# Inputs of a state-space scan: multiplied from replicated token rows on ScalarE and GpSimd in place of TensorE outer products

## What is computed

```python
xc = silu(conv(xa) + conv_b)
Bm = xc @ B_w.T + B_b
Cm = xc @ C_w.T + C_b
A = -exp(clip(A_log, -5, 2))
def step(s, t):
    x_t, b_t, c_t = t
    s = clip(s * A + b_t[:, None, :] * x_t[:, :, None], -10, 10)
    return s, sum(c_t[:, None, :] * s, axis=-1)
```

## Time and profile before

| what | us |
|---|---|
| median of three runs | 1893.89 |
| the profiled execution | 1896.1 |
| its span | 1894.3 |
| TensorE, weight loads | 1524.7 busy, 80% |
| ScalarE | 522.2 busy, 28% |
| GpSimd | 240.0 busy, 13% |
| DMA | 72.65 MB, mean 38 GB/s |

### The profile page before, as it was taken

How to read it: one execution, slowest core, us unless ns; L and a number is a source line. 1 busy time by engine, 2 the same in 40 slices (tenths; PEclk the granted TensorE clock), 3 DMA queues, 4 the chain that set the end, 5 groups by cost and what they waited for, 6 DMA issues and landing times.

```text
span 1894.3 us, 57377 instructions
## 1 busy us (share of the span) xinstructions
PE 1783.8 (94%) x18024; PEld 1524.7 (80%) x18024; DVE 1583.7 (84%) x5997; ACT 522.2 (28%) x1130; POOL 240.0 (13%) x517
## 2 busy tenths in 40 slices
PE   5748779999999999999999999999999999999997
PEld 3434658888888889888888888898888888888886
DVE  5658978989898999989898989899898989898522
ACT  4532103232222223132322223231313232222322
POOL 1010012020111111020202011111102020111100
PEclk9769879999999999999999999999999999999999
DMA  6943100101010101001010101010100101010000
GB/s 191 318 143 108 28 14 14 28 18 31 21 30 20 25 15 36 15 20 30 15 31 21 30 20 30 14 32 15 30 21 18 29 18 31 21 30 9 1 7 6
DMA packets 103435, 72.65 MB, mean 38 GB/s; under 512 B 65384, under 2 KB 95616, under 8 KB 102656
## 3 DMA queue, kind: packets, MB, share of 16 engines
q1 hardware_dynamic: 101936, 67.56, 12.8%
q10 hardware_dynamic: 1232, 1.58, 0.3%
HBM read 45.50 MB, written 23.59 MB: 36 GB/s over the span
## 4 chain that ended last, share of the span: by engine, by line
PE 82%; DVE 1%; issue 1%; ACT 0%; POOL 0%; DVEq 0%; POOLq 0%; ACTq 0%
PE bank L1275 29%; PE bank L1262 24%; PE bank L1176 6%; PE bank L1191 5%; PE bank L1403 3%; PE bank L1350 3%; PE bank L1209 2%; PE bank L1364 2%; PE bank L1357 1%; PE bank L1337 1%; PE bank L1229 1%; PE bank L1383 1%; PE bank L1414 1%; PE bank L1393 1%; DVE x L1759 0%
## 5 line engine op out<-in xcount | busy, mean ns | idle before, releaser
L1646 DVE CUSTOM_DVE_ANT_0 state<-decayed_state,bank 128x128 f32<-128x128 f32 x2048 | 508.3, 287 | 53.4 <-PE bank L1176 48.0
L1636 DVE TENSOR_TENSOR decayed_state<-state,decay 128x128 f32<-128x128 f32 x2048 | 507.1, 287 | 7.6 <-issue 4.2
L1275 PE MATMUL bank<-f_w_sb,hs_whole 128*128 128x256 f32 x2048 | 486.5, 381 | 1.0 <-ACT hs_whole L1058 1.0
L1275 PEld LDWEIGHTS bank<-f_w_sb,hs_whole 128*128 128x128 f32 x2048 | 372.1, 190 | 49.4 <-ACT hs_whole L1058 5.8
L1058 ACT ACTIVATE hs_whole<-bank,f_b_sb 128x256 f32<-128x256 f32 x512 | 214.6, 471 | 650.2 <-PE bank L1262 650.2
L1176 PE MATMUL bank<-xrows,brows 128*128 128x256 f32 x1024 | 252.8, 336 | 39.4 <-DVE state L1646 23.1
L1176 PEld LDWEIGHTS bank<-xrows,brows 128*128 128x128 f32 x1024 | 170.1, 193 | 81.6 <-issue 46.2
L869 POOL TENSOR_TENSOR m_ve<-m_mv,m_eps 128x2 f32<-128x2 f32 x96 | 20.2, 211 | 1237.0 <-DVE m_mv L1673 1237.0
L1262 PE MATMUL bank<-fT_parts,f_w_hi 128*128 128x256 f32 x1024 | 171.2, 290 | 0.7 <-ACT fT_parts L1028 0.7
L1262 PE MATMUL bank<-late_fT_parts,f_w_hi 128*128 128x256 f32 x1024 | 171.5, 290 | 0.0
L1262 PEld LDWEIGHTS bank<-fT_parts,f_w_hi 128*128 128x128 f32 x1024 | 138.4, 189 | 14.0 <-issue 7.0
(11 more groups left out here) (166 smaller groups left out, 2313.3 us busy)
## 6 DMA issues: line engine op xcount, KB each, us to landing
brows<-bs_dram SPq DMA_DIRECT2D x1020, 2.0 KB
xrows<-xs_dram SPq DMA_DIRECT2D x480, 32.0 KB
xt<-in_x SPq DMA_DIRECT2D x4, 1024.0 KB, 7.5
xn_dram<-xn SPq DMA_DIRECT2D x4, 1024.0 KB, 5.8
xs_dram<-xhi SPq DMA_DIRECT2D x8, 512.0 KB, 4.7
xs_dram<-xlo SPq DMA_DIRECT2D x8, 512.0 KB, 5.2
f_w_sb<-in_f_w SPq DMA_DIRECT2D x2, 2048.0 KB
z_dram<-zT SPq DMA_DIRECT2D x8, 512.0 KB, 3.3
```

Of the source, the lines that this page charges most:

```text
L1275: last = pe.matmul(bank_[:, tile * D:(tile + 1) * D], hs_whole[:, slot, m, tile * P:(tile + 1) * P], w(m), start=(m == 0 and tile == 0 and ...
L1636: dve.tensor_tensor(decayed_state[:, part], state[:, (s - 1) % RING, part], decay[:, part], ALU.mult).then_inc(decayed.sem, 1)
L1646: dve._custom_dve(add_sat, out=state[:, s % RING, part], in0=decayed_state[:, part], in1=U[s // 2 % 2][:, s % 2 * D + h * HALF:s % 2 * D + ...
```

## The change

- The scan's inputs are no longer made by TensorE. `scan_inputs` and all `u(n)` calls are gone from its order, and so are `xrows`, `brows` and the PSUM banks `U`.
- SP loads each x row 32 times, once for each state's partition: `xrep` holds 4 slots of 4 steps. `b_steps` holds B as one column per step, loaded for 32 steps at once.
- ScalarE makes the inputs of even steps (a copy with a scale per partition), GpSimd those of odd steps (a multiply by a broadcast column), into `u_ring`, 8 slots in SBUF. Both wait until VectorE has finished step s - 8.
- VectorE's saturating add reads `u_ring`; it waits for ScalarE's or GpSimd's semaphore by parity.
- In the front, `split` is gone, x and B are stored once in full precision, rows are turned in pairs of tiles (four PSUM copies of 512 columns per batch in place of eight of 256), and B's bias is added by ScalarE.
- The hand-written orders of all engines are rearranged.

```diff
+        def load_x_rows(sp, chunk, unit):
             t0 = chunk * CT + unit * USTEPS
             for b in range(B):
+                sp.dma_start(xrep[N_STATE * b:N_STATE * (b + 1), unit % XSLOTS],
+                             g["xs_dram"][b, bass.ds(t0, USTEPS), :].unsqueeze(0).broadcast_to([N_STATE, USTEPS, D])
+                             ).then_inc(x_rows_in[unit % XSLOTS].sem, 16)
...
+                    wait_apart(u_pool_made, u_pool_made.after(i, USTEPS // 2 * (u + 1)))
+                    load_x_rows(sp, i + (u + XSLOTS) // UNITS_U, (u + XSLOTS) % UNITS_U)
+                    if more and u % (UNITS_U // 2) == UNITS_U // 2 - 1:
+                        load_b_steps(sp, i + 1, u // (UNITS_U // 2))
...
+            def scan_input(i, s):
+                unit, n = divmod(s, USTEPS)
+                slot = unit % XSLOTS
+                if not (isinstance(i, int) and i == 0 and s < USLOTS):
+                    pool.wait_ge(stepped.sem, stepped.after(i, 2 * (s - USLOTS + 1)))
+                pool.tensor_tensor(u_ring[:, s % USLOTS], xrep[:, slot, n],
+                                   b_steps[:, s // BSTEPS, s % BSTEPS:s % BSTEPS + 1].broadcast_to([P, D]), ALU.mult).then_inc(u_pool_made.sem, 1)
...
+                act.activation(u_ring[:, s % USLOTS], xrep[:, slot, n], ACT.Copy,
+                               scale=b_steps[:, s // BSTEPS, s % BSTEPS:s % BSTEPS + 1]).then_inc(u_made.sem, 1)
...
-                if s % 2 == 0:
-                    dve.wait_ge(u_made.sem, u_made.after(i, s // 2 + 1))
+                made = (u_made, u_pool_made)[s % 2]
+                dve.wait_ge(made.sem, made.after(i, s // 2 + 1))
...
-                                    in1=U[s // 2 % 2][:, s % 2 * D + h * HALF:s % 2 * D + (h + 1) * HALF],
+                                    in1=u_ring[:, s % USLOTS, part],
```

More of the change, by code:

```diff
@@ L799, in chunk_loads @@
             def chunk_loads(i, more, first=False):
-                for u in range(UNITS_U if more else UNITS_U - GROUPS_U):
+                for u in range(UNITS_U if more else UNITS_U - XSLOTS):
                     if u == TOKENS_AT and not first:
@@ L1132, in step @@
                 gelu(c, 0)
-            step(0, None, None)
+            first_inputs()
+            copy_y(0)
             mlp_high()
@@ L1161, in gates @@
                 last.then_inc(z_made.sem, 1)
-            def scan_inputs(i, n):
-                unit, first = divmod(n, USTEPS // 2)
-                half, q = divmod(unit, GROUPS_U)
-                if n % (USTEPS // 2 * GROUPS_U) == 0:
-                    pe.wait_ge(x_rows_in[half % 2].sem, x_rows_in[half % 2].after(i, 16 * X_DMAS * (half // 2 + 1)))
-                if first == 0:
-                    pe.wait_ge(b_rows_in[q].sem, b_rows_in[q].after(i, 16 * B * (half + 1)))
-                if not (isinstance(i, int) and i == 0 and n < 2):
-                    pe.wait_ge(stepped.sem, stepped.after(i, 4 * (n - 1)))
-                for j in range(2):
-                    tq = (2 * n + j) % USTEPS
-                    last = pe.matmul(U[n % 2][:, j * D:(j + 1) * D], brows[:, q * USTEPS + tq].rearrange("r b n -> r (b n)"),
-                                     xrows[:, half % 2, tq, :], start=True, stop=True)
-                last.then_inc(u_made.sem, 1)
             def scan_output(i, oct_):
@@ L1419, in step @@
                 if c is None and late is None:
[L1420 to L1422 removed]
+                    for n in range(1, CT // 2):
                         for piece in range(2 * KD * B):
@@ L1890, in step @@
                 add_expert(c, 0, 2, res)
+                routing(late, 1)
                 scan(19, 22)
-                routing(late, 1)
                 add_expert(c, 0, 3, res)
-                scan(22, 24)
+                scan(22, 23)
                 add_expert(c, 0, 4, res)
-                scan(24, 26)
+                scan(23, 25)
                 low_half(late, T_FFN2)
-                scan(26, 29)
+                scan(25, 29)
                 add_expert(c, 0, 5, res)
```

466 lines of the change are left out of this document (231 added, 235 removed).

## The result

The change makes the kernel slower: 2047.6 us, the median of four runs (2030.5 to 2050.1), against 1893.89; the ratio of the means is 1.079 with a 95% interval of 1.072 to 1.087. A fourth run of the kernel before, 2280.5 us, fell in a slower state and is not compared. The profiled execution took 2048.6 us with a span of 2046.4.

The account below looks back on a forecast made before the run. VectorE, held up by GpSimd, was to replace TensorE as the bound: period 111.6 us instead of 103.3. From 1896.1, +125 (15 chunks), +9 (chunk 0) and -12 (front) gave 2018, as a median 2016 us; range 1865 to 2090.

Parts of the forecast that it names:

- TensorE relieved, VectorE the bound: Steady state: without 768 matmuls TensorE needs 87.8 us per chunk instead of 103.2, so VectorE sets the period.
- The price of clashes: Scan steps: 22 GpSimd multiplies per chunk each stop VectorE for 0.55 us (0.12 to 0.73), 12.1 us per chunk.
- wide additions: GpSimd's four wide additions per chunk now also stop VectorE's adds, costing 1 us per chunk.
- The exclusion rule: VectorE with two SBUF inputs and GpSimd exclude each other for whole instructions: 16.0 us per chunk, some 64 us above forecast.
- Idle time: VectorE's waits per period: half of today's 9.3 us stays, 4.5 us (ends 2 and 7).
- The rival that put 4 to 5 us of waits on top: Late factor or ReLU per expert stage in ScalarE's and GpSimd's queues: 4 to 5 us per chunk, 2083 us; chance 0.09.
- Chunk 0: First chunk, nothing beside the scan: all 32 multiplies clash, +9 us on 62.3 us.
- The front: Before the scan: removing the split of the rows gives -12 us (ends -3 and -20), limited by transfers.
- ScalarE and DMA: ScalarE's 32 added copies, 14 us per chunk, and replicated row loads, 8.4 MB per chunk, both stay hidden.
- The faster rival: Scan adds escape the exclusion or multiplies fall into VectorE's pauses: period 98.5 us, about 1806 us; chance 0.14.

Follow-up runs that it names:

- the kernel with ScalarE alone: Changed kernel with all 64 scan inputs of a chunk made by ScalarE and none by GpSimd: 1828.4 us, ratio 0.965 to the kernel before.
- beside the kernel before: Kernel before plus 32 idle GpSimd multiplies of 128x256 per chunk into a spare tile, released by the scan's steps: 1924.8 us, ratio 1.015.

## Why the prediction was right, and where it was off

The direction and the term that decides, VectorE held up by GpSimd, were right: 2016 us was forecast, 2048 measured, within the range of 1865 to 2090. That the number came so near is in part luck, because errors cancel: VectorE's busy time came out 3.6 us per period below the 107.1 of the forecast and its idle time 6.9 above; over the 15 chunks 163.7 us were added instead of 125, chunk 0 took 6.6 more than forecast, and the front gave back 13.2 more. By its steps:

- **TensorE relieved, VectorE the bound.** Only half right. The 768 matmuls went, but TensorE was forecast at 87.8 us per period and is busy 103.6 (1243.3 / 12), as much as VectorE (103.5). Of the 15.8 us between, about half is the clock: some 16 us of the period are at the lower level, in which the work of 8 us takes 16. The prediction took a full clock for granted because the steady state before showed 1.00. The other half is a reading: the 15.4 us of the earlier trace rows overlap with other matmuls' records. Without those of L1176 the matmuls of before still cover 98.9 us per period, so only a part of the 15.4 could be won; the kernel with ScalarE alone is at 98.2, with a clock of 0.97. Even at a full clock TensorE would need some 96 us (an estimate: 103.6 less the 8 that the clock costs), not 87.8.
- **The price of clashes.** 22 clashes at 0.55 us, 12.1 us per chunk and 1 for wide additions: 13.1. Measured: 9.5, against the kernel with all inputs on ScalarE 10.1. At the 0.42 us that the clash at 773.31 shows, 22 clashes would make 9.2, and the trace has 24 lengthened operations per chunk more than before, so the count fits and the price was too high. It came from 0.725 us for a multiply, which takes 0.644, and from 0.17 us for the early release alone: the release at 773.7 is 0.14 early, but the decay had also started 0.11 us after the multiply, and that time isn't lost.
- **The exclusion rule.** Adds with two SBUF operands do clash, the step for which no row of before existed; adds with a PSUM operand do not, at 287 ns in both. The Trainium skill (SBUF — State Buffer, "Who interferes with whom") is borne out as to which operations exclude each other. The same page ("SBUF: two separate sides") gives the first to start the ports for the whole instruction. Beside the changed kernel's multiply the trace nearly agrees: the decay is held until 0.14 us before the multiply's recorded end. Beside tile times scalar it doesn't: 0.20 us are lost under 1.16, and operations that start later within it run through. The 16 us that the prediction worked out by that rule would have been 6 too many.
- **Idle time.** 4.5 us forecast (ends 2 and 7), 11.4 measured, outside the ends. This was the largest error of the sum. With the pauses filled it is 5.8 to 6.4, so the term fits once the clock is held. The rival that put 4 to 5 us of waits on top named queued inputs as the cause; there were waits of that size, but they were TensorE's at 1.2 GHz.
- **Chunk 0.** +9 forecast, +15.6 measured; the 6.6 us of difference, and a little more, are the load of the C rows (7.7), which no step looked at.
- **The front.** -12 (ends -3 and -20) forecast, -25.2 measured. The argument that the transfers limit it failed: the last stores of x rows are issued at 88.6 us instead of 109.0 and later, and from 80 to 90 us the DMA share is 0.44 where it was 0.98. The last convolution begins at 72.57 instead of 91.66, 19 us earlier, and most of the gain had arrived by then.
- **ScalarE and DMA** hidden: right. ScalarE's scaled copy takes 505 ns (estimated 430); the replicated rows raise the traffic from 24 to 84 GB/s, and in the steady state no wait for them is in the lists.
- **The faster rival** had its mechanism right for another kernel: without clashes and at 7.1 us of idle time the period is 100.6 and the time 1828, the version with ScalarE alone, which beats both kernels. It named VectorE as the bound; TensorE at 98.2 us stands closer to it.

Of the 11.6 us per period, then, 9.5 are VectorE held up by GpSimd and 2.1 net idle time, in which about 5.6 us of the lower clock hide (11.4 against 5.8), paid in part by waits that went.

What of it stays open: why the price of a multiply is 0.15 us beside the kernel before and some 0.3 in the changed one. Half of the scan's operations are exposed there instead of all, and the trace has 14.9 lengthened decays per chunk, by 0.19 us (median), against 26.0 decays and adds by 0.41. So the clashes are fewer and shorter; what makes them shorter isn't known, as their timing wasn't varied.

## What to carry to other kernels

Before moving elementwise work to GpSimd, count the VectorE operations that read two SBUF operands, and add a stall of each GpSimd operation to VectorE if that is or becomes the bound; an operand left in PSUM, or work given to ScalarE, avoids it. When an engine is relieved, ask what its pauses do: here TensorE lost half of its clock for several microseconds after two pauses of under two, and the engine that waits behind it paid. Before counting on the time of instructions that go, see whether they overlap with those that stay. A busy engine in the profile of before says nothing of its speed after.

## What was not expected of the hardware

- Two pauses of 1.74 and 1.79 us within 5 us were followed by a granted clock of 0.50 over the next 5; 20 matmuls that nobody reads, put into them, made the kernel 77 us (3.8%) faster. The steady state of the kernel before, at 1.00 throughout, doesn't show it, but its front does: from 90 to 98 us TensorE is busy 0.87 us of 8 and the granted clock is 0.50.
- On GpSimd, one tile times one scalar per partition takes 1068 ns for 128x256 (at least 919) where tile times a repeated column takes 644 (at least 607), but stops VectorE for 0.20 us instead of 0.42. The longer instruction gives the faster kernel (1924 against 2048).
- The multiply of the same shape with two whole tiles as operands, beside the kernel before, takes 801 ns on average (at least 718).
